# Padding stores moved to the counting stage, place transfers in sets of 112 and 13 lanes, and the builder's two rows of numbers made one

## The reference

```python
x = _layernorm(x + _L0_gnn_ref(x, ...))   # twice: (x + segment_sum(x[src], dst)) @ W + b
x = _layernorm(x + _L1_gnn_ref(x, ...))   # segment_sum(x[src] + x[dst] + edge_attr_64, dst)
x = _layernorm(x + _L2_gnn_ref(x, ...))   # for each edge: silu(silu([x[src], x[dst], edge_attr_16, w/5] @ ew1 + eb1) @ ew2 + eb2),
                                          # segment_sum over src, then silu([x, agg] @ nw1 + nb1) @ nw2 + nb2 + x
x = _layernorm(x + _L3_gnn_ref(x, ...))   # norm * (x[col] @ W1.T + b1 + x[row]*x[col] @ W2.T + b2), segment_sum over src
```

## Time and profile before

| what | value |
|---|---|
| median of 3 runs | 5745.83 us (5741.8 to 5748.05) |
| the profiled execution: its time, its span | 5754.9 us, 5753.2 us |
| TensorE busy | 4571.3 us (79%) |
| VectorE busy | 2966.1 us (52%) |
| ScalarE busy | 1765.6 us (31%) |
| GpSimd busy | 3327.2 us (58%) |
| DMA, mean over the span | 155 GB/s |

### The profile page before, as it was taken

The page is one execution under the profiler, slowest core; times in us unless marked ns, Lnnn a source line. Parts: engine busy times, 40 slices in busy tenths (PEclk is TensorE's granted clock), DMA queues, the critical chain, the costliest instruction groups (busy, mean ns, idle before and its releaser), DMA issues. The chain is left out here.

```text
span 5753.2 us, 126898 instructions
## 1 busy us (share of the span) xinstructions
PE 4571.3 (79%) x41923; PEld 3947.9 (69%) x41926; DVE 2966.1 (52%) x5201; ACT 1765.6 (31%) x2568; POOL 3327.2 (58%) x3497
## 2 busy tenths in 40 slices
PE   4641699655555359796969999999999999985995
PEld 2320599422222159696948999999999999975995
DVE  6854666777777321313135555555555555534335
ACT  0110000466667720000013333333333333322442
POOL 1004677777777777777007777777777777740000
PEclk9775699989989779698979999999999999987996
DMA  1344577233332379497934444444444444445883
GB/s 52 133 172 171 110 172 169 90 116 113 114 110 105 130 293 419 168 412 272 399 131 118 118 117 118 117 117 118 117 118 118 117 117 117 117 61 108 230 231 81
DMA packets 912337, 892.94 MB, mean 155 GB/s; under 512 B 326543, under 2 KB 814637, under 8 KB 905906
## 3 DMA queue, kind: packets, MB, share of 16 engines
q1 hardware_dynamic: 799776, 725.66, 38.4%
q0 software_dynamic: 112464, 166.06, 11.2%
HBM read 708.70 MB, written 182.60 MB: 155 GB/s over the span
## 5 line engine op out<-in xcount | busy, mean ns | idle before, releaser
L1941 POOL DMA_INDIRECT edge_mlp_b_rows<-b_table,edge_mlp_recs x1664 | 1585.6, 953 | 791.2 <-issue 425.6
L1129 POOL DMA_INDIRECT out_records<-nodes_scatter_recs,nodes_scatter_rows x1650 | 1641.7, 995 | 529.0 <-issue 489.2
L1407 PE MATMUL build_p_ring<-build_hot_near,build_hot_far 128*128 128x392 f16 x2400 | 522.4, 366 | 382.6 <-ACT build_p_ring L1430 198.5
L2064 DVE CAST edge_mlp_hot_t<-edge_mlp_p_turned 128x512 f32<-128x512 bf16 x416 | 287.7, 692 | 836.7 <-PE edge_mlp_p_turned L1987 836.7
L1407 PEld LDWEIGHTS build_p_ring<-build_hot_near,build_hot_far 128*128 128x128 bf16 x2400 | 247.0, 103 | 657.6 <-issue 554.2
L1995 PE MATMUL edge_mlp_p_pre<-edge_mlp_hot_t,edge_mlp_a_blk 128*128 128x128 f32 x3328 | 670.4, 283 | 10.1 <-DMA edge_mlp_b_rows<-b_table,edge_mlp_recs 8.0
L1996 PE MATMUL edge_mlp_p_pre<-c_ident,edge_mlp_b_rows 128*128 128x128 f32 x3328 | 646.0, 276 | 0.0
L1496 PE MATMUL sum_x_p_main<-sum_x_parts,sum_x_tiles 128*128 128x192 bf16 x5488 | 457.6, 247 | 165.4 <-DVE sum_x_parts L1439 165.4
L1964 PE MATMUL edge_mlp_p_m<-edge_mlp_w,edge_mlp_h 128*128 128x128 f32 x3328 | 576.3, 295 | 0.1
L1496 PEld LDWEIGHTS sum_x_p_main<-sum_x_parts,sum_x_tiles 128*128 128x128 f16 x5488 | 456.2, 98 | 166.7 <-issue 166.0
L1307 DVE TENSOR_TENSOR nodes_wide_sums<-nodes_wide_sums,edge_mlp_p_sum 128x128 f32 x1664 | 473.6, 285 | 182.4 <-PE edge_mlp_p_sum L1975 3.9
(11 more groups left out here) (470 smaller groups left out, 6397.8 us busy)
## 6 DMA issues: line engine op xcount, KB each, us to landing
sum_x_tiles<-edge_counts SPq DMA_DIRECT2D x168, 768.0 KB
edge_mlp_a_blk<-a_table SPq DMA_DIRECT2D x1664, 64.0 KB
edge_counts<-build_plane SPq DMA_DIRECT2D x28, 3136.0 KB, 9.6
sum_z_tiles<-edge_counts SPq DMA_DIRECT2D x49, 1792.0 KB
sum_y_tiles<-edge_counts SPq DMA_DIRECT2D x84, 768.0 KB
sums_attr<-in_edge_attr SPq DMA_DIRECT2D x100, 512.0 KB
sum_x_tiles<-edge_counts SPq DMA_DIRECT2D x56, 832.0 KB
out_records<-place_padding SPq DMA_DIRECT2D x104, 256.0 KB
```

Source lines behind the costliest of these rows:

```text
L1129: pool.indirect_dma_start(out=out_rec, out_offset=bass.IndirectOffsetOnAxis(ap=rows[s][:, c:c + 1], axis=0), in_=recs[s][:, c], in_offset= ...
L1407: pe.matmul(p_ring[:, ds(banks[c], 1), 0:KEYS], hot_far[s][:, c // 2, :, c % 2], hot_near[s][:, c // 2, :, c % 2], start=False, stop=True, ...
L1941: pool.indirect_dma_start(out=b_rows[s][:, c], out_offset=None, in_=b_tab, in_offset=bass.IndirectOffsetOnAxis(ap=recs[s][:, c, FE + 1:FE ...
```

## The change

Three edits, which share no data:

1. **Padding.** The tile `padding` is made at the start of `count_out` by GpSimd, ahead of the iota that VectorE needs in that stage. The 4 transfers to `lin_rec` and half of the 104 to `out_rec` are issued in `count_out` by ScalarE's queue, the other 52 by SyncE's. Each queue waits only for the tile. That they have landed is still waited for at the end of `place_out`.
2. **Sets of lanes.** In `place_out` each load of attributes and each store of records becomes two transfers, of lanes 0 to 111 and 112 to 124. Their semaphores count to 32 a piece and not to 16. A scratch tile (`mask`) now lies in a tile that is free then.
3. **One row.** `bank` and `turn` become one row `steps` of 12 words a batch: 8 slots, 2 numbers of pairs, 2 unused. TensorE's queue loads 10 words with one instruction. VectorE writes the row's parts with strides and clears the tile first, and SyncE brings it with one transfer in `plan_windows` where there were two.

The diff, without the lines that only pass arguments on:

```diff
@@ -26,6 +26,7 @@
 WIDE = 75
+LANE_SETS = (0, 112), (112, EP)
 RANKED = 120
@@ -49,6 +50,7 @@
 RING = 6
+STEP_W = 12
 ALIKE = 6
@@ -340,7 +342,7 @@
 
-def count_out(nc, k, a):
+def count_out(nc, k, a, lin_rec, out_rec, padding, prefilled):
 
@@ -354,16 +356,38 @@
         p_row = [ps(f"p_row{q}", [1, 512]) for q in range(2)]
-        number_made, chain = sem("number_made"), sem("chain")
+        number_made, chain, pad_set = sem("number_made"), sem("chain"), sem("pad_set")
         ones_set, hots_made, hots_used = sem("ones_set"), sem("hots_made"), sem("hots_used")
...
         part, pieces, strips = CHUNKS // 4, RANK_W // RANKED, RANKED // STRIP
+        lanes = out_rec[0:P * CHUNKS].rearrange("(p c) w -> p c w", p=P)
         block = st.block()
...
         def _(pool):
+            nc.gpsimd.memset(padding[:], 0.0).then_inc(pad_set, 1)
+            pool.wait_ge(pad_set, 1)
+            nc.gpsimd.memset(padding[:, :, FE + 2:FE + 3], -1.0).then_inc(pad_set, 1)
             nc.gpsimd.iota(number[:], [[P, CHUNKS]], base=0, channel_multiplier=0).then_inc(number_made, 1)
+
+        @block.scalar
+        def _(act):
+            act.wait_ge(pad_set, 2)
+            spare = lin_rec[EP * EC:EP * EC + (P - EP) * EC // P * P].rearrange("(p c) w -> p c w", p=P)
+            for lo in range(0, (P - EP) * EC // P, PRE):
+                width = min(PRE, (P - EP) * EC // P - lo)
+                act.dma_start(spare[:, lo:lo + width], padding[:, 0:width]).then_inc(prefilled, 16)
+            beyond = (P - EP) * EC % P
+            act.dma_start(lin_rec[P * EC - beyond:P * EC], padding[0:beyond, 0]).then_inc(prefilled, 16)
+            for i in steps(act, CHUNKS // (2 * PRE)):
+                act.dma_start(lanes[:, ds(i * (2 * PRE), PRE)], padding[:]).then_inc(prefilled, 16)
+
+        @block.sync
+        def _(sp):
+            sp.wait_ge(pad_set, 2)
+            for i in steps(sp, CHUNKS // (2 * PRE)):
+                sp.dma_start(lanes[:, ds(i * (2 * PRE) + PRE, PRE)], padding[:]).then_inc(prefilled, 16)
 
@@ -606,8 +630,7 @@
         base, chunk_no = sb("base", [P, IT]), sb("chunk_no", [P, IT], I32)
-        turned_t, turned_x = sb("turned_t", [IT, P], I32), sb("turned_x", [XB, 2, P // WIN], I32)
-        turns_t = sb("turns_t", [IT, P // HALF], I32)
+        steps_t, turned_x = sb("steps_t", [IT, P // BATCH, STEP_W], I32), sb("turned_x", [XB, 2, P // WIN], I32)
         moved = [sb(f"moved{q}", [P, P]) for q in range(2)]
@@ -654,12 +677,11 @@
             sp.wait_ge(rows_out, 2)
-            sp.dma_start(k["bank"][:], turned_t[:]).then_inc(rows_in, 16)
-            sp.dma_start(k["turn"][:], turns_t[:]).then_inc(rows_in, 16)
+            sp.dma_start(k["steps"][:], steps_t[:]).then_inc(rows_in, 16)
             sp.wait_ge(rows_out, 4)
...
             sp.dma_start(k["x_col"][:], turned_x[:, 1]).then_inc(rows_in, 16)
-            sp.wait_ge(rows_in, 112)
+            sp.wait_ge(rows_in, 96)
 
@@ -831,8 +853,10 @@
             dve.wait_ge(turned, 1)
-            dve.tensor_copy(turned_t[:], p_turn[0:IT, 0]).then_inc(rows_out, 1)
-            dve.tensor_copy(turns_t[:], p_turn[0:IT, 1, HALF - 1::HALF]).then_inc(rows_out, 1)
+            step(dve.memset(steps_t[:], 0))
+            dve.tensor_copy(steps_t[:, :, 0:BATCH], p_turn[0:IT, 0].rearrange("i (b c) -> i b c", c=BATCH)).then_inc(rows_out, 1)
+            dve.tensor_copy(steps_t[:, :, BATCH:BATCH + BATCH // HALF],
+                            p_turn[0:IT, 1, HALF - 1::HALF].rearrange("i (b c) -> i b c", c=BATCH // HALF)).then_inc(rows_out, 1)
             dve.wait_ge(b_turned, 1)
@@ -936,13 +960,12 @@
 
-def place_out(nc, k, a, lin_rec, out_rec, ea16, in_rec):
+def place_out(nc, k, a, lin_rec, ea16, in_rec, prefilled):
 
...
         sb, ps, sem, sems = st.sb, st.ps, st.sem, st.sems
-        padding = sb("padding", [P, PRE, OUT_REC])
         attr = [sb(f"attr{s}", [EP, WIDE, FE]) for s in range(2)]
@@ -950,10 +973,10 @@
         rest, behind = [sb(f"rest{h}", [P, NB], FP16) for h in range(2)], sb("behind", [EP, NB])
-        spread, mask, back = sb("spread", [P, P], FP16), sb("mask", [EP, EP]), sb("back", [EP, EP], BF16)
+        spread, mask, back = sb("spread", [P, P], FP16), a.run[:, 0:EP], sb("back", [EP, EP], BF16)
         p_rank = [ps(f"p_rank{h}", [P, BY, 512]) for h in range(2)]
         ranks_asked, ranked, taken = sem("ranks_asked"), sem("ranked"), sem("taken")
-        pad_set, prefilled, chain, spare_set = sem("pad_set"), sem("prefilled"), sem("chain"), sem("spare_set")
+        chain, spare_set = sem("chain"), sem("spare_set")
         cleared, attr_in, made, stored = sem("cleared"), *([sem(f"{n}{s}") for s in range(2)] for n in ("attr_in", "made", "stored"))
@@ -973,14 +996,16 @@
                         sp.wait_ge(made[j % 2], 4 * (j // 2))
-                    sp.dma_start(attr[j % 2][:], attrs[:, j * WIDE:(j + 1) * WIDE]).then_inc(attr_in[j % 2], 16)
+                    for lo, hi in LANE_SETS:
+                        sp.dma_start(attr[j % 2][lo:hi], attrs[lo:hi, j * WIDE:(j + 1) * WIDE]).then_inc(attr_in[j % 2], 16)
 
...
                     sp.wait_ge(made[j % 2], 4 * (j // 2 + 1))
-                    sp.dma_start(lines[0:EP, j * WIDE:(j + 1) * WIDE], recs[j % 2][:]).then_inc(stored[j % 2], 16)
+                    for lo, hi in LANE_SETS:
+                        sp.dma_start(lines[lo:hi, j * WIDE:(j + 1) * WIDE], recs[j % 2][lo:hi]).then_inc(stored[j % 2], 16)
 
@@ -988,18 +1013,8 @@
                 assemble(ea16)
-            sp.wait_ge(pad_set, 2)
-            spare = lin_rec[EP * EC:EP * EC + (P - EP) * EC // P * P].rearrange("(p c) w -> p c w", p=P)
-            for lo in range(0, (P - EP) * EC // P, PRE):
-                width = min(PRE, (P - EP) * EC // P - lo)
-                sp.dma_start(spare[:, lo:lo + width], padding[:, 0:width]).then_inc(prefilled, 16)
-            rest = (P - EP) * EC % P
-            sp.dma_start(lin_rec[P * EC - rest:P * EC], padding[0:rest, 0]).then_inc(prefilled, 16)
-            lanes = out_rec[0:P * CHUNKS].rearrange("(p c) w -> p c w", p=P)
-            for i in steps(sp, CHUNKS // PRE):
-                sp.dma_start(lanes[:, ds(i * PRE, PRE)], padding[:]).then_inc(prefilled, 16)
             for s in range(2):
-                sp.wait_ge(stored[s], 16 * ((pieces + 1 - s) // 2))
+                sp.wait_ge(stored[s], 32 * ((pieces + 1 - s) // 2))
             sp.wait_ge(prefilled, 16 * (CHUNKS // PRE + 1 + -(-((P - EP) * EC // P) // PRE)))
@@ -1008,11 +1023,11 @@
                 if j >= 2:
-                    act.wait_ge(stored[s], 16 * (j // 2))
+                    act.wait_ge(stored[s], 32 * (j // 2))
                 act.mul(recs[s][:, :, FE], a.weight[:, at], 1.0 / CUTOFF).then_inc(made[s], 1)
...
                 act.copy(recs[s][:, :, FE + 2], a.low[:, at]).then_inc(made[s], 1)
-                act.wait_ge(attr_in[s], 16 * (j // 2 + 1))
+                act.wait_ge(attr_in[s], 32 * (j // 2 + 1))
                 act.copy(recs[s][:, :, 0:FE], attr[s][:]).then_inc(made[s], 1)
@@ -1043,9 +1058,6 @@
                 nc.gpsimd.memset(recs[s][:], 0.0).then_inc(cleared, 1)
-            nc.gpsimd.memset(padding[:], 0.0).then_inc(pad_set, 1)
-            pool.wait_ge(pad_set, 1)
-            nc.gpsimd.memset(padding[:, :, FE + 2:FE + 3], -1.0).then_inc(pad_set, 1)
             nc.gpsimd.iota(a.row[:], [[1, EC]], base=P * CHUNKS - EP * EC, channel_multiplier=EC).then_inc(spare_set, 1)
@@ -1391,12 +1403,14 @@
                 for s in range(BATCHES):
-                    _, banks = nc.values_load_multi_w_load_instructions(
-                        k["bank"][0:1, ds(it * (BATCH * BATCHES) + s * BATCH, BATCH)], engines=[PE], min_val=0,
-                        max_val=RING - 1, skip_runtime_bounds_check_because="its low bits")
-                    _, turns_of = nc.values_load_multi_w_load_instructions(
-                        k["turn"][0:1, ds(it * (BATCH * BATCHES // HALF) + s * (BATCH // HALF), BATCH // HALF)], engines=[PE],
-                        min_val=1, max_val=ALL_SLOTS // 2, skip_runtime_bounds_check_because="a pair of slots' number and one")
+                    _, values = nc.values_load_multi_w_load_instructions(
+                        k["steps"][0:1, ds(it * BATCHES + s, 1), 0:BATCH + BATCH // HALF].rearrange("o b v -> o (b v)"), engines=[PE],
+                        min_val=0, max_val=ALL_SLOTS // 2, skip_runtime_bounds_check_because="banks, and numbers of pairs of slots")
+                    banks = [nc.s_assert_within(v, min_val=0, max_val=RING - 1, skip_runtime_bounds_check_because="its bank")
+                             for v in values[:BATCH]]
+                    turns_of = [nc.s_assert_within(v, min_val=1, max_val=ALL_SLOTS // 2,
+                                                   skip_runtime_bounds_check_because="a pair of slots' number and one")
+                                for v in values[BATCH:]]
                     if s % 2 == 1:
@@ -2280,8 +2294,8 @@
```

(10 more changed lines are left out.)

## The result

The changed kernel takes 5604.8 us (5598.9 to 5608.4), the one before 5745.2 us beside it: a ratio of 0.9756, 95% interval 0.9742 to 0.9771. It is 140 us faster, where 259 were forecast (5487 us). The profiled execution took 5608.4 us, its span is 5606.8.

What follows compares the result with a forecast made beforehand. SyncE's padding issues bound the place stage's tail and TensorE's queue the builder. Savings of 94 us in front and 165 in the builder made 259: 5754.9 to 5496 profiled, 5487 us median; own range 5462 to 5520, wider 5462 to 5560.

Steps and rivals of the forecast that it cites:

- Padding: Stages in front: moving it takes 102.9 us off the place stage's tail and lengthens the counting stage by 9 us.
- Sets of lanes: Place stage: pieces move at 337 GB/s instead of 132, so the stage ends with VectorE; value 0, bound +15 us.
- One register load: Builder, TensorE's queue: two more words cost 0.015 us; quiet batch 2.59 to 2.01 us, builder 902 to 722, saving 180.
- a load of ten words above 0.65 us: Builder: a register load of 10 words taking longer than this was listed as a sign that the forecast is wrong.
- The stretches with slow loads: Builder, about 8 us at each plane: two or three slow loads instead of four, 3.0 us x 24.4 = 73 us.
- the 28 us allowed for chains that meet: Builder: TensorE's 694 us and VectorE's 692 won't run together at 694; 4% added, giving 722 us.
- The rival by the word: Builder: a load's time grows with its words, builder stays at 902 us, total 5652; 7%, shared with no builder gain.
- The rest of the builder: Builder: shorter batches save 180 us, of which 165 count because GpSimd's scatter has only 176 us of slack.
- The ring: Builder: TensorE waits until ScalarE clears the pair 3 before; builder 800 us, saving 100, total 5552; chance 25%.
- Scatter: Block's end: if the builder reaches 700 us, GpSimd's scatter is last; 94 + 172 = 266, 5480 us; within the forecast's 62%.

Runs made afterwards that it cites:

- e7_one_queue: Changed kernel with bank and turn loaded separately again, & 4095 on the builder's wait numbers, all padding issued by SyncE alone in the counting stage: 5731.5 us in one run.
- e6_padding_only: Changed kernel with bank and turn loaded separately again, & 4095 on the builder's wait numbers, without the lane sets: 5737.7 us, ratio 0.9989.
- e3_words: Builder with & 4095 on wait numbers; a turn's six batches load their ten numbers six ways, from 48-byte rows: 5773.8 us in one run.
- e10c_turn_once: Changed kernel with separate bank and turn loads, & 4095 on wait numbers, a turn's twelve turn numbers in one load; third try: 5538.8 us, ratio 0.9638.
- c_after: Changed kernel with one AND (& 4095, value unchanged) on each number TensorE and ScalarE wait for in the builder: 5655.1 us, ratio 0.9829.
- e11c_best: Sets only, padding behind the pieces, twelve turn numbers in one load a turn, TensorE's ANDs (& 4095) on these together; third try: 5613.7 us, ratio 0.9776.

## Why the prediction was wrong, point by point

*Padding: right in what it adds.* Queues, rate and end: 379 GB/s forecast, 373 to 380 measured; the place stage was to begin 9 us later and begins 8.1 later. With one queue it is 327 GB/s at a share of 0.86 (e7_one_queue), with two 373 at 1.02, so the second gives the idle share, as the row of one queue (337 GB/s at 0.89) allowed.

*Sets of lanes: right in the sum, not in the split.* 94 us forecast for both, 94.4 in the trace, 91 by the ratios. The prediction gave the whole of it to the padding's move and priced the sets at 0, at most 15. The runs show the sets worth 24 us once the padding is moved and 103 without that, and the padding's move a loss of 10 once the sets are there. It took the last piece's chain to end 6 us behind VectorE's and its store to land in 9.3 us; in e6_padding_only it landed 24 us behind. That the sets would carry the pieces at 337 GB/s was the author's estimate, which no row of before shows; with them the pieces moved at 330, without them at 133 (e6_padding_only).

*One register load: this step failed.* It says "7.5 ns a word, 0.015 us", a straight line through 592 ns for eight words and 547 for two. Two sizes can't show steps: both were two accesses, and ten words are four. The prediction had named a load of ten words above 0.65 us as a sign that it was wrong. Measured, 1.081 us is 0.47 over the forecast 0.607, 142 us over 300 batches. Not all of it was lost: the load that went gave more than the 0.58 counted for it, so a quiet batch took 2.40 and not 2.01, 117 us over 300. The stretches with slow loads took 109 us (846.8 less 300 x 2.40 + 18) and not 73, since the ten-word loads in them grow from 1.08 to about 3.5; the 28 us allowed for chains that meet were not needed. 117 + 36 - 28 is the shortfall of 125 in the builder.

The rival by the word had the better mechanism: a word that is not one of an aligned four costs an access of 0.24 to 0.27 us (e3_words). It fails for aligned fours: there four registers took 335 ns together. I weighed it down with the eight-word row, which held two fours. Its time, 5652, was missed all the same, since the ten words still save a load: 5604.8. Of the 0.19 us that a quiet batch gained, the durations explain 0.06 (1.139 less 1.081); the rest is the address operation and the gaps that went with the load.

*The rest of the builder: right as far as tested.* With loads nearly as cheap as the prediction thought (e10c_turn_once: 0.73 us a batch on the mean, against 0.607) the builder gains 170 us, against 165 to 180 forecast, though from 956 to 786 with the ANDs and not from 902 to 722. That the two numbers are so near is partly luck, since it is another edit. The ring doesn't hold the builder: a turn got shorter by about what TensorE's queue was spared, while ScalarE's work stayed the same (0.81 to 0.82 and 0.81 us a pair). TensorE's waits for ScalarE (198.5 us before, 122.8 after, 120.4 in e10c_turn_once) can't show it: with the ANDs alone they rise to 194.1 in c_after.

*Scatter.* Its last is through at 2649, 125 us ahead of the block's end: it never became the bound, so the case in which it would was not tested.

## What to carry to other kernels

The register loads from SBUF tried here are priced by accesses of about a quarter of a microsecond: begun at a multiple of 16 bytes, one for each full four words and one for each word left over (0.335 us for four words, 0.599 for eight, 0.857 for twelve, 1.088 for ten); begun 8 bytes behind one, one for each word (1.478 us for six, 1.968 for eight). So pad rows to fours, align them, and take numbers that several steps share in one aligned load. Don't trade a load for work that lets TensorE stand still between matmuls: behind a gap of 3.88 us its granted clock fell from 1.00 to 0.50 (e11c_best). Where two rows of a trace give a price at two sizes, ask which steps they could hide before drawing a line through them. And when two edits remove the same tail, try each alone: here one of them did more alone than both together.

## What the runs showed that I had not expected

- On SBUF rows a load of twelve words (0.857 us) is faster than one of ten (1.088), and eight words that begin 8 bytes off an aligned four take 1.968 us instead of 0.599.
- A load that is taken out, with its address operation, gives 0.16 us more than its own duration; an AND of 32 ns costs 0.09 us in TensorE's sequencer, and 0.16 with its move.
- Twelve ANDs in a row lengthened TensorE's gap from turn to turn by 1.93 us, and the granted clock behind a gap of 3.88 us fell to 0.50: two batches of 2.59 and 2.46 us in place of 1.90.
- On two of the chips every kernel, the one before too, took 7558 to 7840 us (medians), with address operations of up to 1.4 us in TensorE's sequencer; the cause is open.
